# One head in eight of a mixing loop: two products on TensorE, or one product of a sum made by VectorE

## The reference

```
dtA = A * dt[:, None]                               # 128 heads x 64 states
Cc  = Bc[None, :, :] * Cc * (exp(dtA) - 1.0) / A    # 32 x 128 x 64, complex
V   = exp(dtA[:, :, None] * ell)                    # ell = 0 .. 1023
K   = 2.0 * einsum('chn,hnl->chl', Cc, V).real      # 32 x 128 x 1024
```

## Time and profile before

| | us |
|---|---|
| median of the runs | 1650.8 |
| the profiled execution, its own time | 1653.0 |
| its span | 1651.2 |
| PE busy in the span | 1565.5 (95%) |
| PEld busy | 1245.3 (75%) |
| DVE busy | 1192.9 (72%) |
| ACT busy | 882.5 (53%) |
| POOL busy | 689.1 (42%) |
| mixing loop on PE, first to last product | 43.3 to 164.6 (start of the last one) |

### The profile page before, as it was taken

The page is one execution under the profiler, slowest core; times in us unless marked ns, Lnnn a source line. Parts: engine busy times, 40 slices in busy tenths (PEclk is TensorE's granted clock), DMA queues, the critical chain, the costliest instruction groups (busy, mean ns, idle before and its releaser), DMA issues. The chain is left out here.

```text
span 1651.2 us, 35437 instructions
## 1 busy us (share of the span) xinstructions
PE 1565.5 (95%) x11810; PEld 1245.3 (75%) x11810; DVE 1192.9 (72%) x2175; ACT 882.5 (53%) x2926; POOL 689.1 (42%) x687
## 2 busy tenths in 40 slices
PE   4999699999999999999999999966999999999996
PEld 2999577888888888888888888855677777777774
DVE  8787576667676767666676666664798888888885
ACT  7796236777777777777777777772111111111110
POOL 0993064444444444444444444421333333333333
PEclk8999799999999999999999999988999999999999
DMA  8455421010101010101010110222233332333221
GB/s 216 103 142 140 143 75 40 27 52 25 51 27 49 32 44 32 44 32 44 32 44 32 44 38 26 89 104 87 77 108 112 114 108 93 104 114 113 92 87 45
DMA packets 59513, 123.19 MB, mean 75 GB/s; under 512 B 9441, under 2 KB 30178, under 8 KB 59458
## 3 DMA queue, kind: packets, MB, share of 16 engines
q1 hardware_dynamic: 59458, 122.47, 23.6%
HBM read 71.71 MB, written 51.66 MB: 75 GB/s over the span
## 5 line engine op out<-in xcount | busy, mean ns | idle before, releaser
L855 POOL TENSOR_TENSOR pr<-pr,ri 128x512 f32<-128x512 f32 x256 | 266.3, 1040 | 487.4 <-DVE ri L1281 487.4
L1114 ACT ACTIVATE pr<-sm,ml 128x128 f32<-128x128 f32 x1024 | 399.5, 396 | 33.6 <-DVE ml L1274 32.6
L945 PE MATMUL att_ps<-w_lo,xT_hi 128*128 128x512 f32 x792 | 337.1, 426 | 0.0
L945 PE MATMUL att_ps<-w_hi,xT_lo 128*128 128x512 f32 x792 | 314.5, 397 | 0.0
L945 PE MATMUL att_ps<-w_hi,xT_hi 128*128 128x512 f32 x792 | 313.5, 396 | 0.0
L1265 DVE TENSOR_TENSOR sm<-att_ps,cst 128x512 f32<-128x512 f32 x256 | 173.0, 676 | 135.9 <-PE att_ps L1008 135.9
L1128 ACT COPY pT<-att_ps 128x512 f32<-128x512 f32 x256 | 149.5, 584 | 165.9 <-PE att_ps L1017 165.9
L1541 PE MATMUL ffn_o<-wo_hi,cT_hi 128*128 128x512 f32 x528 | 217.1, 411 | 3.8 <-DVE cT_lo L1592 3.8
L1541 PE MATMUL ffn_o<-wo_hi,cT_lo 128*128 128x512 f32 x528 | 207.8, 393 | 0.0
L1541 PE MATMUL ffn_o<-wo_lo,cT_hi 128*128 128x512 f32 x528 | 207.1, 392 | 0.0
L1114 ACT ACTIVATION_READ_ACCUMULATOR pr<-sm,ml 128x1 f32 x1024 | 196.8, 192 | 0.0
(11 more groups left out here) (204 smaller groups left out, 2510.7 us busy)
## 6 DMA issues: line engine op xcount, KB each, us to landing
h_in<-h_rows SPq DMA_DIRECT2D x33, 512.0 KB, 4.3
h_rows<-ho SPq DMA_DIRECT2D x64, 256.0 KB, 3.9
hbuf<-h_rows SPq DMA_DIRECT2D x32, 512.0 KB, 3.6
ctx_turned<-ctxo SPq DMA_DIRECT2D x64, 256.0 KB, 2.0
ctx_in<-ctx_turned SPq DMA_DIRECT2D x32, 512.0 KB, 3.5
out_dram<-yo SPq DMA_DIRECT2D x32, 512.0 KB, 2.7
raw<-in_L_attn_Wq_dram SPq DMA_DIRECT2D x8, 512.0 KB, 17.8
w_raw<-in_L_ffn_w_dram SPq DMA_DIRECT2D x4, 1024.0 KB, 5.2
```

The costliest lines, as they stand in the source:

```text
L855: G.tensor_tensor(pr[:, g % 4], pr[:, g % 4], ri[:, g % 2, :].unsqueeze(2).to_broadcast([P, GQ, P]), ALU.mult).then_inc(p_ready, 1)
L945: mm = nc.tensor.matmul(bank[:], x_part[:, t[1], e, tok:tok + P], w_part[blk][:, e, :], start=(r == 0), stop=(r == EC * 3 - 1))
L1114: a = nc.scalar.activation(pr[:, g % 4, q, :], sm[:, g % 2, q, :], ACT.Exp, bias=ml[:, b[1], 0, h:h + 1], accum_out=ml[:, b[1], 1, h:h + 1])
```

## The change

In each half, the last head (`SUMMED`, number 7 of 0 to 7) is treated in another way. After both product tiles of the half DVE waits for its own product (`products`), adds the 8 blocks by 32 channels of that head, `m1 = m1 + m2` (128x256, f32, both operands and the result in SBUF), and signals `sums`. PE waits for `sums` ahead of that head and then makes one product per half of its blocks where it made two.

```diff
+    sums = sem("sums")
...
+    SUMMED = CH - 1
...
                     for e in range(2):
+                        h = 2 * i + e
+                        terms = (m1,) if h == SUMMED else (m1, m2)
+                        if h == SUMMED:
+                            pe.wait_ge(sums, 2 * k + half + 1)
                         for jj in range(2):
-                            h = 2 * i + e
                             slots = slice(jj * (JB // 2), (jj + 1) * (JB // 2))
                             cols = slice((2 * e + jj) * PB, (2 * e + jj + 1) * PB)
-                            for term in (m1, m2):
+                            for term in terms:
                                 mm = nc.tensor.matmul(bank[:, cols],
                                                       term[:, half, h, slots].rearrange("p j c -> p (j c)"),
                                                       eb[:, k % 3, half * CH + h, :],
-                                                      start=term is m1, stop=term is m2)
+                                                      start=term is m1, stop=term is terms[-1])
...
             t.then_inc(products, 1)
+            v.wait_ge(products, 2 * k + half + 1)
+            V.tensor_tensor(m1[:, half, SUMMED], m1[:, half, SUMMED], m2[:, half, SUMMED], ALU.add).then_inc(sums, 1)
```

## The result

The changed kernel takes 1654.07 us (median of 22 runs, 1652.30 to 1656.43) against 1651.47 us of the kernel before (22 runs beside them, 1650.59 to 1653.54). The ratio is 1.0015, with a 95% interval of 1.0009 to 1.0022: 2.5 us slower, between 1.5 and 3.6. The profiled execution took 1654.88 us over a span of 1653.1, 1.9 us more than the one of before.

A forecast was written before the change was run, and what follows sets the result against it. The prediction took the ring of POOL's phases and subtraction and DVE's rounding to bound the loop's second half. Stops of +3.25 and -0.5 at the loop's end gave +2.75 us on 1650.8, say 1653.6, range 1650.9 to 1656.2.

The forecast's parts named there:

- the ring: Mixing loop's second half: DVE's rounding, POOL's subtraction and sixteen phases take 14.82 us per turn and pace PE's 14.35.
- The additions stop POOL: In the ring: 13 additions with both operands in SBUF each stop POOL 0.25 us, so the last rounding comes 3.25 later.
- the seam: Between POOL's subtraction and next instruction: a group's second addition may fall there, near 125.7 us, and cost less.
- my price: POOL's stop per addition in the ring: 0.25 us, bounded by zero and 0.42, near the 0.26 scaled from L495.
- The longer stop: Rival in the ring: over 0.29 us per addition, up to 0.42, giving +5.0 and 1655.8 us; chance 0.30.
- DVE's time behind the additions: On DVE: each addition delays what follows by 0.45 us; the wait before L500 shrinks from 2.50 to about 1.4.
- the sum: Whole kernel: +3.25 from the ring and -0.5 at the loop's end make +2.75 us.
- PE waits for nothing in its added wait: On PE ahead of the summed head: the sum is ready 6.3 us of PE work early; cost zero.
- The loop's end: After the last rounding: the last group starts 0.4 us later, its two halves save 0.9; net -0.5.
- What follows the loop: Behind the last bank copy: the chain through `cls_sb` has no slack, so what the loop loses arrives whole.
- PE's clock: PE in the loop: 88% busy should keep full clock; rival, it falls to 1.2 GHz, +6, 1656.8 us, chance 0.05.
- The signs: Profile after: additions 0.42 us, sixteen phases 9.2, L500 starts 15.3 apart, PE waits about 1 us each half.

The follow-up runs named there:

- e1: Changed kernel without the additions and PE's wait, PE still making one product for the last head; ratio 0.9995 to the kernel before.
- e5: Kernel before, with DVE instead of POOL writing the phases of three of a group's 16 heads ahead of the rounding; ratio 0.9989.
- e2: Changed kernel with the additions going to a tile nobody reads and PE making both products for every head; ratio 1.0020 to the kernel before.
- e3: Changed kernel with the additions' second operand taken from PSUM in the first seven groups; ratio 0.9999 to the kernel before.
- e8: Changed kernel with four heads of eight summed instead of one, additions of 128x1024; ratio 1.0066 to the kernel before.
- e4: Changed kernel with the addition and saved products only in the second half of each group; ratio 1.0010 to the kernel before.
- e9: Changed kernel with the addition and saved products only in the first half of each group; one run, 15.10 us per turn.

## Why the prediction held, point by point

**The bound.** Right: the ring of POOL's phases, subtraction and DVE's rounding. e1 and e5 show it from both sides: products taken from PE buy 1.0 us, and work taken from POOL removes PE's pauses.

**The additions stop POOL.** Right in kind and cause (e2, e3, e8). The size was off. The term was 13 x 0.25 = 3.25 us; the last rounding came 2.54 later, 13 x 0.195. In the first group, where the addition stands by itself, it cost 0.28 in L345's row; the first rounding starts 7.41 after the first tile, against 7.11 before and 7.18 in e1 and e3. In the six full turns the pair cost 2.24 / 6 = 0.37 and not 0.50. One reason is in the rows: beside the second addition L345 lost 0.18 and not 0.25, and 0.19 us of that addition lay ahead of the phase, at the seam that I had given as a reason for less before taking 0.25 all the same. The rest of the difference stays open, since e4 and e9, with one addition per turn, gave 0.26 and 0.24, which is my price. The longer stop, which would have made it clearly slower, did not come. Its argument was that POOL loses a start between an addition and the L500 that follows at once; e9 has just these additions, and at 0.24 per turn they cost no more than those that stand apart in e4.

The Trainium skill (SBUF — State Buffer, section "SBUF: two separate sides") restricts the contention to VectorE operations with two SBUF inputs or in a two-port mode. e3 agrees: with one operand in PSUM the stop is gone. That POOL loses a whole instruction's time is not what the rows show: of the 0.30 us that L345 at 82.06 shares with the addition it lost 0.18, of the 1.10 us in e8 0.99, and in the first group 0.28 beside an addition of 0.48.

**DVE's time behind the additions.** I had 0.45 us each. What follows starts 0.38 (71.56 to 71.94) and 0.42 (81.87 to 82.29) after the addition; to that come 0.03 of waiting and the overlap of 0.08 with the product ahead, which the wait takes away (four products of 2.28 took 8.87 in the earlier trace rows). So it was about 0.5. I had left out that overlap, and taken the 0.42 from rows ahead of the loop, where POOL wrote no phases; beside them the additions are up to 0.1 longer. DVE's wait for POOL shrank to 1.91, not 1.4: the stop that lengthens the ring gives part of it back, 14.86 to 15.23, which I had left out of that number though not out of the sum.

**PE waits for nothing in its added wait.** Right: PE's idle time names the tiles `m` of L606 and `eb` of L500, 7.9 and 5.0 us, and no addition. Its waits per turn are 0.74 and 0.56 us, where I had said about 1 each.

**The loop's end.** Right: -0.5 predicted, 2.07 - 2.54 = -0.47 measured. The parts fit too: PE's last group starts at 150.39, 13.25 behind the last rounding, against 140.58 + 7.17 = 147.75 before, 12.84 behind, so 0.4 later, as forecast; its two halves then save 0.9.

**What follows the loop.** Right: last copy +1.8 and span +1.9 in the profiled execution.

**PE's clock.** It was 1.00 from 50 to 160 us in the changed kernel, as forecast, with PE busy 88% of a turn (120 records at 0.112 in 15.23 us); in e8, with 64% (96 records in 16.83), it fell.

**The signs.** One was stated wrongly: a phase of sixteen was to last 9.2 us, and it lasts 9.35. That sign counted the first addition alone, though the sum has both of them in the ring, and the starts 15.3 apart as well.

**The time.** Forecast +2.75, measured 2.5 (1.5 to 3.6) over the median beside it; 1653.6 against 1654.07, as the kernel before itself came out 0.7 higher beside it than in its first three runs. That +2.5 lies so near to +2.75 is in part luck: the one execution in which the loop can be measured lost 2.07 in it, 0.7 less than the sum says, and the interval holds both. The mechanism is what e2 and e3 confirm; the price of 0.25 was too high by a fifth for this kernel.

## What to carry to other kernels

Before moving work from the busiest engine, look for waits that come back once per turn between the others: here TensorE was 98% busy in its loop and still followed a ring of GpSimd and VectorE, and the saved products became waiting. On that ring a short VectorE instruction with both inputs in SBUF costs twice: VectorE's own time, which a wait covered here, and a stop of GpSimd that grows with the columns, 0.00105 us each; one input in PSUM avoids the stop. When the true bound was relieved first (three phases moved), the same change no longer lost 2.5 us; that it gains anything of its own there is not shown.

## What I had not expected

The instruction that is stopped does not start late. It starts on time in the profile and lasts longer (0.62 instead of 0.44 us beside 256 columns, 1.43 beside 1024), so the start of the phases behind L351 hides the stop; the duration of the one instruction shows it.

In e8 the granted clock fell in the middle of a loop that works in even portions, to a mean of 0.79 between 110 and 130 us, with PE busy 15.06 of 20 us, part of that at the lower clock.
